# Folding latent weights two heads at a time, and running the routed layers' tail in halves

## What is computed

```python
def _L1_ffn_ref(x, attention_mask, position_ids, router_w, ...):   # the routed layer, called twice
    weights = (x @ router_w)[..., 0] + router_b[0]
    topv, topi = jax.lax.top_k(weights, k)                 # k = 64 of 512 tokens, 63 are taken
    sel_idx = jnp.sort(topi[:, :kc], axis=1)
    x_sel, w_sel = x[bidx, sel_idx], weights[bidx, sel_idx]
    hn = rmsnorm(x_sel, ln1)                               # then q, k, v with 16 heads of 16, rope
    sc = jnp.einsum('bhqd,bhkd->bhqk', q, kk) / np.sqrt(hd) + m_sel[:, None]
    a = jax.nn.softmax(sc, axis=-1)
    o = jnp.einsum('bhqk,bhkd->bhqd', a, v)...reshape(b, kc, d) @ wo
    x1 = x_sel + o
    x2 = x1 + jax.nn.gelu(rmsnorm(x1, ln2) @ w1) @ w2      # 256 -> 1024 -> 256
    out = jnp.zeros_like(x).at[bidx, sel_idx].set(x2 * w_sel[..., None])
    return out + x * (1.0 - sel_mask)[..., None]

def _L1_attn_ref(x_bld, Wq, Wkv_down, Wk_up, Wv_up, Wout): # the latent attention, 16 heads of 64
    q = jnp.einsum('bld,dhk->blhk', x_bld, Wq)
    latent = jnp.einsum('bld,dc->blc', x_bld, Wkv_down)    # 64 latent features
    k = jnp.einsum('blc,chk->blhk', latent, Wk_up)
    v = jnp.einsum('blc,chk->blhk', latent, Wv_up)
    ...
    return jnp.einsum('bqhd,hdo->bqo', y, Wout)
```

## Time and profile before

| | |
|---|---|
| median of 3 runs | 2855.82 us (2855.44 to 2856.29) |
| the profiled execution | 2856.62 us, its span 2854.4 us |
| TensorE matmul busy | 2490.6 us, 87% |
| VectorE busy | 2105.5 us, 74% |
| ScalarE busy | 1573.0 us, 55% |
| GpSimd busy | 877.8 us, 31% |

### The profile page before, as it was taken

One profiled execution on the slowest core, in us unless ns is written; L12 is line 12 of the kernel. 1 busy time (PEld: TensorE's weight loads), 2 busy tenths in 40 slices (PEclk: granted clock), 3 DMA queues, 4 the chain that ended last, 5 costly groups with the idle time before them and its releaser, 6 DMA issues. The chain is left out here.

```text
span 2854.4 us, 39741 instructions
## 1 busy us (share of the span) xinstructions
PE 2490.6 (87%) x14369; PEld 1354.2 (47%) x14369; DVE 2105.5 (74%) x3896; ACT 1573.0 (55%) x2523; POOL 877.8 (31%) x857
## 2 busy tenths in 40 slices
PE   7999999989999999999999777588888888898376
PEld 3444444444444444444444455255555555565254
DVE  3489688878879886888814455689779878877754
ACT  6655454545555554545554442277667767766251
POOL 4444343434443443444445500102112212202200
PEclk9999999999999999999999678699999999999677
DMA  5100000000000000000000100000000000000101
GB/s 181 54 1 1 0 1 1 1 1 1 1 1 1 1 1 1 1 1 1 1 1 1 49 16 0 1 2 2 2 3 2 2 2 2 2 2 1 49 16 59
DMA packets 29167, 33.09 MB, mean 12 GB/s; under 512 B 6404, under 2 KB 25396, under 8 KB 28964
## 3 DMA queue, kind: packets, MB, share of 16 engines
q1 hardware_dynamic: 27988, 27.88, 3.0%
q0 software_dynamic: 976, 2.56, 0.3%
HBM read 25.58 MB, written 4.19 MB: 10 GB/s over the span
## 5 line engine op out<-in xcount | busy, mean ns | idle before, releaser
L757 POOL TENSOR_TENSOR g_lo<-g_full,g_hi 128x512 f16<-128x512 f32 x512 | 670.5, 1313 | 900.6 <-ACT g_hi L849 899.0
L849 ACT ACTIVATE g_full<-hid,b_col 128x512 f32<-128x512 f32 x512 | 351.8, 687 | 562.2 <-PE hid L152 560.8
L150 PE MATMUL hid<-y_hi,w_hi 128*128 128x512 f16 x1024 | 396.9, 388 | 39.2 <-DVE y_lo L835 34.9
L151 PE MATMUL hid<-y_lo,w_hi 128*128 128x512 f16 x1024 | 396.0, 387 | 0.0
L152 PE MATMUL hid<-y_hi,w_lo 128*128 128x512 f16 x1024 | 395.3, 386 | 0.0
L150 PE MATMUL acc<-g_hi,w_hi 128*128 128x512 f16 x1024 | 389.5, 380 | 5.2 <-POOL g_lo L757 5.2
L151 PE MATMUL acc<-g_lo,w_hi 128*128 128x512 f16 x1024 | 389.4, 380 | 0.0
L152 PE MATMUL acc<-g_hi,w_lo 128*128 128x512 f16 x1024 | 389.2, 380 | 0.0
L849 ACT ACTIVATE g_hi<-hid,b_col 128x512 f16<-128x512 f32 x512 | 349.1, 682 | 0.0
L2139 DVE TENSOR_REDUCE mla_m_col<-mla_ps 128x1 f32<-128x512 f32 (+3 forms) x512 | 224.9, 482 | 62.2 <-PE mla_ps L1981 56.5
L2277 ACT ACTIVATE mla_p_full<-mla_ps 128x1280 f32<-128x1280 f32 x128 | 158.4, 1237 | 144.9 <-PE mla_ps L2011 144.6
(11 more groups left out here) (371 smaller groups left out, 4910.6 us busy)
## 6 DMA issues: line engine op xcount, KB each, us to landing
latent_stage<-in_L_ffn_w_dram SPq DMA_DIRECT2D x16, 512.0 KB, 4.7
x<-in_L_attn_x_dram SPq DMA_DIRECT2D x8, 512.0 KB, 8.5
routed_w<-in_L_ffn_w_dram SPq DMA_DIRECT2D x4, 1024.0 KB, 7.7
out_dram<-x SPq DMA_DIRECT2D x8, 512.0 KB, 4.8
mla_sums<-mla_sum_row SPq DMA_DIRECT2D x128, 2.0 KB
latent_stage<-in_L_attn_Wq_dram SPq DMA_DIRECT2D x1, 1024.0 KB, 8.5
latent_stage<-in_L_attn_Wout_dram SPq DMA_DIRECT2D x1, 1024.0 KB, 10.7
routed_wqkv<-in_L_ffn_wq_dram SPq DMA_DIRECT2D x2, 256.0 KB, 2.9
```

Of the source, the lines that this page charges most:

```text
L150: pe.matmul(out, w_hi, v_hi, start=first, stop=False)
L151: pe.matmul(out, w_hi, v_lo, start=False, stop=False)
L757: pool.tensor_tensor(g_lo[:, g, :], g_full[:, g, :], g_hi[:, g, :], ALU.subtract).then_inc(tail_done, 1)
L849: act.activation(out[:, g, :], hid[:, ht % 4, :], ACT.Gelu, bias=b1_col[:, ht:ht + 1], scale=1.0 / WS).then_inc(gelu_done, 1)
```

## The change

It has three parts.

**The fold, two heads at a time.** `wk_t` and `wv_t` become block-diagonal: the two heads of a pair stand in different columns, with zeros (two memsets on GpSimd, at the head of its stream) where a head has nothing. So one product over 128 rows gives both heads, and one bank of PSUM holds a pair; four pairs can be in flight in place of two. The copies out of `turn` are four of 64 partitions in place of two of 128, those of a pair are two in place of four, and a pair's copies now stand before every batch of the norm. Two pairs are folded ahead of the router's transposes and six behind, all ahead of L1309's transposes.

**One exponential for a pair.** VectorE subtracts the maximum over 128x1024 elements (in place of the negation of 128x16), ScalarE takes one exponential over 128x1024, and VectorE sums the rows (a reduction of 128x1024, in `divide`).

**Halves.** The second norm, turn, up, gelu and down are done for pairs 0 and 1 and then for pairs 2 and 3. The first half's norm comes before the last two quotients on VectorE, and its turn before the last pair's `turn_p` on TensorE; products of the last pairs stand between the first half's up slices. The first two put-backs stand between the second half's up and down, and the pass-through instructions are spread between the others.

```diff
-        self.wk_t = sb("wk_t", [P, MLA_PAIRS, LATENT])
+        self.wk_t = sb("wk_t", [P, MLA_PAIRS, 2, LATENT])
...
     def fold(self, pe, m):
...
-        if m >= 2:
-            pe.wait_ge(self.fold_out, m - 1)
-        for i in range(2):
-            bank = self.bank(m, i)
-            rows = slice(i * MLA_DIM, (i + 1) * MLA_DIM)
-            for k in range(KD):
-                pe.matmul(self.ps[:, bank, k * LATENT:(k + 1) * LATENT], self.wq_t[rows, m, k * P:(k + 1) * P],
-                          self.wk_t[rows, m, :], start=True, stop=True)
-            last = pe.matmul(self.ps[i * LATENT:(i + 1) * LATENT, bank, D:2 * D], self.wv_t[rows, m, :],
-                             self.wout[rows, m, :], start=True, stop=True)
-        last.then_inc(self.folded, 1)
+        if m >= 4:
+            pe.wait_ge(self.fold_out, m - 3)
+        bank = self.bank(m)
+        for k in range(KD):
+            pe.matmul(self.ps[:, bank, k * P:(k + 1) * P], self.wq_t[:, m, k * P:(k + 1) * P],
+                      self.wk_t[:, m, :, :].rearrange("p i c -> p (i c)"), start=True, stop=True)
+        pe.matmul(self.ps[:, bank, D:2 * D], self.wv_t[:, m, :, :].rearrange("p i c -> p (i c)"), self.wout[:, m, :],
+                  start=True, stop=True).then_inc(self.folded, 1)
...
+    def clear(self, pool):
+        for w in (self.wk_t, self.wv_t):
+            pool.memset(w[:, :, :, :], 0.0).then_inc(self.cleared, 1)
...
-            dve.tensor_scalar(mx, mx, -1.0, None, ALU.mult).then_inc(s_step, 1)
+            dve.tensor_tensor(sv, sv, mx.unsqueeze(2).to_broadcast([P, HEADS, ROWS]), ALU.subtract).then_inc(s_step, 1)
...
             dve.wait_ge(s_exp, pr + 1)
+            dve.tensor_reduce(total, s[:, pr % 2, :, :], AX.X, ALU.add).then_inc(sum_step, 1)
...
-                    for hd in range(HEADS):
-                        last = act.activation(s[:, pr % 2, hd, :], s[:, pr % 2, hd, :], ACT.Exp,
-                                              bias=s_col[:, pr % 2, 0, hd:hd + 1],
-                                              accum_out=s_col[:, pr % 2, 1, hd:hd + 1])
-                    last.then_inc(s_exp, 1)
+                    act.activation(s[:, pr % 2, :, :], s[:, pr % 2, :, :], ACT.Exp).then_inc(s_exp, 1)
...
+        def up(pe, a, part):
+            pe.wait_ge(h_out, KD + KD * (a + 1))
+            for f in range(4 * part, 4 * part + 4):
+                if f >= 3:
+                    pe.wait_ge(gel_out, FFN // P * a + f - 2)
+                for k in range(KD):
+                    last = pe.matmul(up_slot(a, f), w1[:, k, f * P:(f + 1) * P], h_t[:, k, half_cols(a)],
+                                     start=(k == 0), stop=(k == KD - 1))
+                last.then_inc(up_done, 1)
+
+        def down(pe, a, i):
+            for f in range(FFN // P):
+                if i == 0:
+                    pe.wait_ge(gel_out, FFN // P * a + f + 1)
+                pr = HALF * a + i
+                last = pe.matmul(ps[:, DOWN_BANK[a], i * D:(i + 1) * D], gel[:, f, pr * P:(pr + 1) * P],
+                                 w2[:, f, :], start=(f == 0), stop=(f == FFN // P - 1))
+            last.then_inc(down_done, 1)
...
+                up(pe, 0, 0)
+                project(pe, 2)
+                turn_o(pe, 3)
+                up(pe, 0, 1)
+                project(pe, 3)
+                down(pe, 0, 0)
+                down(pe, 0, 1)
+                turn_half(pe, 1)
+                up(pe, 1, 0)
+                up(pe, 1, 1)
+                put(pe, 0)
+                put(pe, 1)
+                down(pe, 1, 0)
+                put(pe, 2)
+                down(pe, 1, 1)
+                for b in range(3, BATCH):
+                    put(pe, b)
...
+                add_and_square(1)
+                scale_half(0)
+                divide(dve, 2)
+                pass_by(0)
+                divide(dve, 3)
+                add_and_square(2)
+                add_and_square(3)
+                scale_half(1)
+                for b in (1, 2, 3):
+                    pass_by(b)
+                processed(0)
+                processed(1)
+                put_back(0)
+                put_back(1)
+                pass_by(4)
+                pass_by(5)
+                put_back(2)
+                pass_by(6)
+                pass_by(7)
+                processed(2)
+                processed(3)
+                for b in range(3, BATCH):
+                    put_back(b)
```

205 lines of the change are left out of this document (111 added, 94 removed).

## The result

| | median us | single times | against before, 95% interval |
|---|---|---|---|
| before | 2856.06 | 2855.44 to 2856.61 | |
| changed kernel | 2814.68 | 2811.18, 2812.27, 2817.08, 2820.47 | 0.9857, 0.9839 to 0.9876 |
| forecast | 2815 | 2803 to 2828 | |

The changed kernel takes 41.4 us less. In the two profiled executions it is 45.4 us less (2856.62 and 2811.18); the one of after is the fastest of its four, which spread over 9.3 us, before's over 1.2.

The account below looks back on a forecast made before the run. TensorE was taken to bound the fold stage, alternating engines the attention, a serial chain the tail. Savings of 16.5 + 23.4 + 1.0 = 40.9 us from 2856.62 leave 2815.7 profiled, 2815 median; range 2803 to 2828.

Parts of the forecast that it names:

- Fold, -16.5 forecast: First routed layer's first block: fold products hide under VectorE's pick, saving 16.5 us, between 13 and 18.
- the give-back: Behind the fold block: 0.5 us lost again for a gather on a TensorE that has idled longer.
- 1.74 us at the low clock: Fold on TensorE: a pair costs 1.74 us at clock 0.50, eight pairs 13.9 in place of 33.3.
- rival (c): Fold block: GpSimd bounds it, splits slowed to 2.7 us each give 5 us back, 2820 us; chance 0.10.
- the terms of 1.5 and 0.5: VectorE in the fold block: 1.5 us of GpSimd's holding regained, 0.5 given back for splits under the pick's end.
- Routed layers, -23.4 forecast: Attention and tail of both routed layers: 83.7 us in place of 95.45, 11.7 less in each, 23.4 in all.
- rival (b): Attention: denser work lifts TensorE to the high clock, 5 us a layer less, 2805 us; chance 0.15.
- Rival (e): Routed layers: exponentials' time returns as VectorE time, halves only move waits, fold alone counts, 2839 us; chance 0.05.
- Output, -1.0 forecast: Output transfers: five in place of eight come 1.13 us apart, the last waits 1.0 us less, between 0 and 2.
- VectorE pausing more than 7 us in the attention: Attention: a sign that would show the forecast wrong, VectorE pausing more than 7 us there.
- (d): Routed layers: clock stays low to the end of the first half's down, 14 us more each, 2843 us; chance 0.08.
- (f): Tails of both routed layers: low clock holds throughout, 62 us more in all, 2877 us; chance 0.03.

Follow-up runs that it names:

- after_again: The changed kernel, unchanged, in more executions on the chip of later runs: 2815.68 us, 42.1 less than the original.
- fold_only: Original kernel with only the fold's part (block-diagonal products, new places, zeroing on GpSimd), attention and tail as before: 2843.35 us.
- fold_old_place: Changed kernel with the full-row fold products in the original's places, six pairs behind the router's transposes, two behind the picked rows' turn: 2823.91 us.
- exp_only: Original kernel with only one exponential a pair (subtraction and row sum on VectorE): 2833.47 us.
- fold_exp: Changed kernel without the halves: new fold and one exponential a pair; norm, feed-forward and put-back of all pairs in one piece: 2818.83 us.
- halves_old_exp: Changed kernel with the original's sixteen exponentials a pair, new fold and halves kept: 2822.53 us.
- warm: Changed kernel with ten more 128x128 identity transposes in TensorE's pause ahead of the first half's turn: 2807.23 us.
- swap: Changed kernel with pair 3's probabilities turned ahead of the first half's turn on TensorE, copies on ScalarE likewise: 2812.86 us.
- tail_order: Changed kernel with VectorE's pass-throughs moved earlier and put 3 ahead of the last down projection: 2810.19 us.
- fold_64: Changed kernel with the original's 64-row fold products (two halves a pair), in the changed kernel's places: 2821.55 us.
- warm_more: Changed kernel with the edits of warm and tail_order, plus 14, 4 and 8 transposes before the picked rows' turn, gather and pair 0's turn: 2799.33 us.

## Why the prediction was right, and where it was not

**The sum.** 40.9 us forecast, 41.4 measured (42.1 in the second set). The range held. The three terms did not all keep their size. In the profiles the fold brings 15.1 us (16.5 forecast), the two walks 27.9 in after and 22.9 in after_again (23.4), the output 1.2 and 1.3 (1.0): 44.2 and 39.3. So the forecast lies between an execution with the high level in one walk and one without. That the medians came within 1.2 us of it is in part luck: the fold fell 1.4 us short and the level, which no term of the sum had, made up for it.

**Fold, -16.5 forecast.** The block shrank by 16.7 us, L1768 came at 1622.18 (forecast 1621.1, and 0.83 of the difference is the later start of the block). But the give-back was 1.7 us where I had 0.5, and what is left to the first score shift is 15.1. Alone, in fold_only, the part measures -13.0 by medians and -15.1 in profiles: inside -13 to -18, at its edge. The step "1.74 us at the low clock" had the price right and the level wrong: where full-row products did run at the low level they took 1.70 us a pair (fold_old_place), but in after all eight pairs ran at the high one, 0.88 us. It cost nothing, since the pick covered either. It did decide that no pair came near the end, so rival (c) had less ground than I gave it: GpSimd ended at 1621.0 and VectorE closed the block 0.9 us later.

**VectorE's holding.** From L85 to the end of the pick it is 29.9 us (1590.59 to 1620.48), 30.7 before: 0.8 regained where the terms of 1.5 and 0.5 said 1.0. L85 takes 0.19 here, no longer 1.39. The statistics lay under the two memsets (1588.76 to 1590.60) and took 1.41 us for four, and in before, with only short GpSimd instructions beside them, this:
```profile
1587.97 1.41 DVE L232 BATCH_NORM_STATS2 router_stats<-x 128x6 f32<-128x256 f32 x4 [2.46 <-PEq L2404]
```
So the row agrees with the Trainium skill, SBUF — State Buffer, "SBUF: two separate sides", by which, as the prediction read it, the memsets cost the statistics under them nothing.

**Routed layers, -23.4 forecast.** Walk 1 follows the forecast step by step: exponential 0 to 5.0 (forecast 5.0), projection 0 to 21.0 (20.7), first half's norm 30.9 (30.65), values 3 to 38.1 (37.8), down 56.9 (55.8), processed rows 0 and 1 by 62.4 (61.5), end 84.7 (83.7). Walk 2 left it at values 1 (1.85 us in place of 3.22), so shift 3 began at 19.9 (forecast 22.1), and it ended 5.6 us below the forecast, the size of rival (b); so the level differs between layers and executions of one kernel. Where the gain comes from was not in the forecast, which priced exponentials and halves as one term. exp_only, fold_exp and halves_old_exp show it: the exponential alone gives 22.9 us, and the halves 3 to 4 more by medians, over times that overlap. Rival (e) was wrong on the exponentials, which did not come back as VectorE time, and nearly right on the halves, which at the low clock mostly moved waits. What I expected of the exponential alone in exp_only, 7.3 us a layer, was too low as well: 11.4 came. TensorE's work behind the attention is the same, it starts with slow slices, and 5 put-backs in place of 8 stand at the end while 16 pass-throughs that were free are now on VectorE's path.

**Output, -1.0 forecast.** From the last put-back to the end of the span it is 8.0 us (2801.23 to 2809.2), before 9.2: -1.2. Landing is 3.6 in the median, before 4.8.

**A sign that I had named.** VectorE pausing more than 7 us in the attention was to show me wrong. It was idle for 6.6 of the 31.65 us up to the turn of pair 3, and then for 6.82 us more ahead of pair 2's addition. So the sign came, yet the end did not move: my walk had those waits in its steps and not in the sentence.

**Rivals (d) and (f)** fell: from the fourth up slice on the projections of after run at their short durations (four slices 3.6 us, the down projection 7.07), and 1727 to 1740 was granted 1.00.

**What stays open.** The rows of warm and after show that the clock level in and behind the attention makes the difference between them. Why one walk of after gets the high level in the attention by itself (0.69 in the window) and three don't, no run tells; the second walks of swap and tail_order, built on it, got it too. Nor does any run tell what varies between executions of before.

## What to carry to other kernels

Two edits that each remove the same wait don't add: price each alone and on top of the other before both are written, since here the smaller edit (one exponential a pair) brings 24.5 of the 28.7 us between fold_only and after, and the larger one (halves) the rest, if it is clear of noise at all. Two products over half the rows each cost more than one over all rows: at the high level a pair took 2.29 us in halves (fold_64, 1593.09 to 1595.38) and 0.88 in one. So zeros in a block-diagonal operand were cheap: two memsets of 0.95 us on GpSimd. Where TensorE pauses ahead of a dense stretch, look at the granted clock before and behind the pause. Here it was high before and low behind, and a few added transposes into a free bank were worth 8.4 us, twice as much as the halves. And compare stretches from the start of their own block: absolute times of two executions differ by what happened before the edit.

## What the runs showed of the hardware

- Under products over 64 rows the granted clock fell from 1.00 to 0.50 though TensorE was never idle (fold_64: a pass of 256 columns 0.29 us at first, later 0.52), and before's stayed at 0.50 for 24.00 of 24.00 us. Full-row products in before's place ran at 1.00 at 4.00 of 4.00 us busy (fold_old_place), and in after at 8.37 of 12.40.
- The high level was lost over a pause of 2.76 us in after, and kept over 1.51 us left behind ten 128x128 transposes that themselves ran at it (1.31 us): from 1700 to 1740 warm was granted 1.00. Eight transposes in a pause that began at the low level ran low, and so did the turn and the values right behind them.
- The first layer's gather of 64 products took 11.19 to 11.23 us in nine kernels with the new products, and 9.44 in warm_more, with 18 transposes ahead. Behind the same idle 19.4 us the second layer's took anything from 9.80 to 11.37, so a pause alone does not fix it.
- An exponential over 128x1024 takes 1.057 us in one instruction and 5.42 in sixteen.
